# Delta-rule attention with its longest convolution as products with diagonal matrices and its level 0 written down directly, unused products at TensorE's waits, and the first block of keys loaded and projected in halves

## The reference

```python
q = short_conv_silu(hidden_states @ Wq, conv_q_w)   # causal, 4 taps per column; k and v alike
beta = sigmoid(hidden_states @ Wb)
q, k = l2norm(q), l2norm(k); v = v * beta; kb = k * beta
attn = -(kb @ k.T) * strict_lower
for i in range(1, chunk):                            # forward substitution: (I + A)^-1
    attn[i, :i] += attn[i, :] @ attn[:, :i]
u = (attn + eye) @ v
delta_out = ((q @ k.T) * incl_lower) @ u
outs = [dwconv_causal(v_direct, w) for w in (ms_w3, ms_w15, ms_w31)]   # 3, 15 and 31 taps per column
ms_out = (concat(outs) @ kernel_mix_w) @ channel_mixer_w
gate_features = concat([hidden_states, mean|ms_out|, mean|delta_out|, mean|v_direct|])
logits = gelu(gate_features @ fusion_w1 + fusion_b1) @ fusion_w2 + fusion_b2
wts = softmax(logits over the 3 branches)
o = wts0 * ms_out + wts1 * delta_out + wts2 * v_direct
return (o * rsqrt(mean(o * o)) * o_norm_w) @ Wo
```

## Time and profile before

| | |
|---|---|
| median of 3 executions | 2513.3 us (2511.05 to 2516.91) |
| profiled execution, its own time | 2525.92 us |
| its span | 2524.0 us |
| mean granted TensorE clock, share of full speed | 0.926 |
| busy: PE, DVE, ACT, POOL | 90%, 68%, 59%, 16% |

### The profile page before, as it was taken

How to read it: one execution, slowest core, us unless ns; L and a number is a source line. 1 busy time by engine, 2 the same in 40 slices (tenths; PEclk the granted TensorE clock), 3 DMA queues, 4 the chain that set the end, 5 groups by cost and what they waited for, 6 DMA issues and landing times. The chain is left out here.

```text
span 2524.0 us, 67781 instructions
## 1 busy us (share of the span) xinstructions
PE 2276.3 (90%) x26335; PEld 1850.0 (73%) x26335; DVE 1704.4 (68%) x4080; ACT 1485.1 (59%) x2976; POOL 408.0 (16%) x347
## 2 busy tenths in 40 slices
PE   6999999778999999998567899999975999999949
PEld 5888888676777777776543788888854788888738
DVE  5777777437888888887743577777744677777632
ACT  3666666535777777776113366666642666666621
POOL 3222221002212212120000122222102222222000
PEclk9999999888999999999557899999976999999959
DMA  6776676265443443431113766766614766767426
GB/s 137 121 121 119 120 122 106 49 204 149 112 120 92 120 105 103 125 85 42 30 60 107 143 97 117 119 114 118 103 29 110 139 121 119 122 119 121 64 84 209
DMA packets 150490, 277.47 MB, mean 110 GB/s; under 512 B 32654, under 2 KB 70367, under 8 KB 150251
## 3 DMA queue, kind: packets, MB, share of 16 engines
q1 hardware_dynamic: 150252, 274.13, 52.8%
HBM read 118.86 MB, written 0.33 MB: 47 GB/s over the span
## 5 line engine op out<-in xcount | busy, mean ns | idle before, releaser
L1132 DVE TENSOR_REDUCE L3x_tops<-L3x_m_bank 128x1 f32<-128x448 f32 x448 | 262.6, 618 | 126.6 <-PE L3x_m_bank L904 124.3
L1132 DVE TENSOR_REDUCE L2x_tops<-L2x_m_bank 128x1 f32<-128x448 f32 x448 | 262.6, 618 | 123.2 <-PE L2x_m_bank L904 120.8
L454 ACT ACTIVATE L1x_prob<-L1x_p_s,L1x_neg_max 128x512 f32<-128x512 f32 (+1 forms) x400 | 274.9, 687 | 119.4 <-DVE L1x_neg_max L565 116.6
L1132 DVE TENSOR_REDUCE L0x_tops<-L0x_m_bank 128x1 f32<-128x448 f32 x448 | 262.4, 618 | 122.3 <-PE L0x_m_bank L904 120.2
L560 DVE CUSTOM_DVE_ANT_0 L1x_p_s<-L1x_p_s,L1x_mask 128x512 f32<-128x512 f32 (+1 forms) x400 | 273.4, 684 | 37.8 <-PE L1x_p_s L320 32.6
L1037 ACT ACTIVATE L2x_prob<-L2x_s_bank 128x512 f32<-128x512 f32 x448 | 219.4, 542 | 94.3 <-PE L2x_s_bank L915 92.9
L1037 ACT ACTIVATE L0x_prob<-L0x_s_bank 128x512 f32<-128x512 f32 x448 | 219.4, 542 | 91.8 <-PE L0x_s_bank L915 90.6
L1037 ACT ACTIVATE L3x_prob<-L3x_s_bank 128x512 f32<-128x512 f32 x448 | 219.4, 542 | 90.8 <-PE L3x_s_bank L915 89.5
L329 PE MATMUL L1x_p_t<-net_ident,L1x_prob 128*128 128x128 f32 x1568 | 239.7, 274 | 11.7 <-ACT L1x_probT L175 11.6
L329 PEld LDWEIGHTS L1x_p_t<-net_ident,L1x_prob 128*128 128x128 f32 x1568 | 192.9, 141 | 49.7 <-ACT L1x_probT L175 13.5
L320 PE MATMUL L1x_p_s<-L1x_k_stack,L1x_q_stack 96*128 96x512 f32 (+1 forms) x400 | 182.7, 458 | 1.8 <-DVE L1x_q_stack L544 1.8
(11 more groups left out here) (720 smaller groups left out, 4494.6 us busy)
## 6 DMA issues: line engine op xcount, KB each, us to landing
L0x_k_stack<-L0x_kT SPq DMA_DIRECT2D x336, 112.0 KB, 4.0
L2x_k_stack<-L2x_kT SPq DMA_DIRECT2D x336, 112.0 KB, 4.0
L3x_k_stack<-L3x_kT SPq DMA_DIRECT2D x336, 112.0 KB, 4.0
L1x_k_stack<-L1x_kT SPq DMA_DIRECT2D x288, 128.0 KB, 2.4
L3f_w<-in_L_ffn_w SPq DMA_DIRECT2D x16, 1024.0 KB, 9.3
L0x_ctx<-in_ctxT SPq DMA_DIRECT2D x14, 896.0 KB
L2x_ctx<-in_ctxT SPq DMA_DIRECT2D x14, 896.0 KB
L3x_ctx<-in_ctxT SPq DMA_DIRECT2D x14, 896.0 KB
```

The costliest lines, as they stand in the source:

```text
L454: e.activation(prob[:, h % P_RING, 0:nk], p_s[h % S_RING][:, 0:nk], ACT.Exp, bias=neg_max[:, odd, h:h + 1]).then_inc(sem("exped"), 1)
L1132: e.tensor_reduce(tops[:, b % 2, h, half:half + 1], m_bank[n % RING][:, 0:HALF], AX, ALU.max).then_inc(sem("m_free"), 1)
```

## The change

It has three parts. In what follows line numbers of the changed kernel are given only where an order of instructions is shown.

**The delta-rule attention.**
- K is projected first, then V, then Q; Wk comes by SP, Wv and Wq by DMAs that ACT issues after its square root. K and V are convolved on DVE as before, Q on POOL with 7 TENSOR_TENSORs of 256 elements per partition. K is normed alone before the levels, Q within them (levels 2 and 3); the local matrix is made in level 5.
- The 31-tap convolution leaves DVE. POOL spreads the taps into 62 diagonal matrices `diag` (4 TENSOR_TENSORs of 2048, 1920, 2048 and 1920 elements per partition), and PE adds up 62 products of a diagonal matrix with the shifted `vpad` in one bank. They are placed between the other products of the levels. DVE keeps 18 taps, spread 1, 1, 2, 4, 5, 5 over the levels.
- Level 0 has no products: `XT = I - BT`, turned once by PE for `X`. Six levels remain. The copy to `Y` goes from DVE to ACT. `X` is updated, and the next `B·X` released, once `X·Y` alone is there. The last level makes no `X`.
- The `fw1` products (8, with one product of zeros to open the bank) move from the tail into level 1. Gelu is followed piece by piece by its `fw2` product, and the means of sizes are made one by one.

**Unused products.** `keep_busy` multiplies the identity with itself, n times 128x128, into a bank that nobody reads at the time, ahead of a wait of PE: 4 + 9 in each turned cross attention's prologue, 4 + 7 in L1x, 4 + 6 + 5 in L0a and L2a, 4 + 3 + 8 in L0f, 4 + 6 + 3 in L1f, 4 + 6 + 20 + 8 in L1a, 4 + 5 + 12 + 8 in L2f, 14 + 4 + 9 in L3a, 4 + 10 in L3f.

**The prologue of the turned cross attention.** Block 0 comes by two DMAs of 448 keys and is split in halves; the pieces are projected in the order 0, 2, 1, 3, the first two when the first half is split. The split of wv moves from ACT and DVE to POOL, ahead of the split of block 1. Three of the six `k_stack` DMAs of quad 0 of block 0 are issued by ACT, three stay with SP.

```diff
@@ turned cross attention, SP, POOL, PE, ACT, DVE
-                elif b:
-                    e.wait_ge(sem("ctx_0_split"), 1)
...
-                    for r in range(2):
+                    for r in range(1 if b == 0 and j == 0 else 2):
...
-            load(0)
+            for half in range(2):
+                keys = slice(half * HALF, (half + 1) * HALF)
+                e.dma_start(ctx[:, :, keys], ctx_dram[:, :, keys]).then_inc(sem(f"ctx_0_loaded_{half}"), 16)
...
+            e.wait_ge(sem("v_weights"), 16)
+            e.tensor_copy(wv_part[:, HIGH], wv).then_inc(sem("v_weights_high"), 1)
...
             split_ctx(1)
...
+            keep_busy(e, p_oT, ident, 9)
             e.wait_ge(sem("k_weights_split"), 1)
-            e.wait_ge(sem("ctx_0_split"), 1)
-            for i, bank in enumerate([p_proj] + m_bank):
-                project(0, i, bank)
+            for n, bank in enumerate([p_proj] + m_bank):
+                e.wait_ge(sem("ctx_0_split"), 1 + n // 2)
+                project(0, FIRST_KEYS[n], bank)
...
+            e.wait_ge(sem("k_split"), 4)
+            for n, (_, part) in enumerate(PRODUCTS):
+                at, of = GROUP + HD * n, HD
+                e.dma_start(k_stack[at:at + HD, 0, 0::4, :].bitcast(F32),
+                            kT[of:of + HD, 0, part].bitcast(F32)).then_inc(sem("k_stacked_0_0"), 16)
@@ helper
+def keep_busy(e, bank, ident, n):
+    for _ in range(n):
+        e.matmul(bank[:, 0:P], ident[:], ident[:], start=True, stop=True)
@@ delta_rule_attention, POOL
+            def spread_taps(g):
...
+                e.tensor_tensor(diag[:, c, at:at + n, :], ident[:].unsqueeze(1).broadcast_to([P, n, P]),
+                                taps[2][:, c, at:at + n].unsqueeze(2).broadcast_to([P, n, P]),
+                                ALU.mult).then_inc(sem("diag_made"), 1)
+            e.wait_ge(sem("taps_loaded"), 16)
+            spread_taps(0)
...
+            e.wait_ge(sem("pre_copied"), 3)
+            for j in range(4):
...
+                    link(e.tensor_tensor(tapped[:], src, over, ALU.mult))
+                    link(e.tensor_tensor(conv[:, Q], conv[:, Q], tapped[:], ALU.add))
...
+            for g in range(1, 4):
+                spread_taps(g)
@@ delta_rule_attention, PE
+            def spread(first, last):
+                for k in range(first, last):
...
+                    t = e.matmul(bank[5][:, c * P:(c + 1) * P], diag[:, c, j, :], vpad[:, c, j:j + P],
+                                 start=j == 0, stop=j == TAPS[2] - 1)
...
+            keep_busy(e, bank[7], ident, 20)
+            e.wait_ge(sem("k_activated"), 1)
...
-            for level in range(LEVELS):
-                e.wait_ge(sem("B_masked"), level + 1)
+            for level in range(1, LEVELS):
...
+                    e.wait_ge(sem("X_updated"), level - 1)
...
+                if level < LAST:
+                    for h in range(NH):
+                        t = e.matmul(bank[1][:, h * P:(h + 1) * P], XT[:, h, :], Y[:, h, :], start=True, stop=True)
+                    t.then_inc(sem("XBX_made"), 1)
...
+                if level == 1:
+                    e.wait_ge(sem("loop_weights"), LOOP)
+                    e.matmul(bank[7][:], nothing[:, 0:P], nothing[:], start=True, stop=False)
+                    for oc in range(HC):
...
@@ delta_rule_attention, ACT and DVE
+                e.wait_ge(sem("BX_made"), level)
+                e.copy(flat(Y), bank[4][:]).then_inc(sem("BX_copied"), 1)
...
-                e.wait_ge(sem("XBX_made"), level + 1)
-                e.wait_ge(sem("XBXT_made"), level + 1)
-                link(e.tensor_tensor(flat(X), flat(X), bank[1][:], ALU.subtract))
+                if level < LAST:
+                    e.wait_ge(sem("XBX_made"), level)
+                    e.tensor_tensor(flat(X), flat(X), bank[1][:], ALU.subtract).then_inc(sem("X_updated"), 1)
+                e.wait_ge(sem("XBXT_made"), level)
+                e.tensor_tensor(flat(XT), flat(XT), bank[0][:], ALU.subtract).then_inc(sem("XT_updated"), 1)
```

More of the change, by code:

```diff
@@ L1786, in _ @@
[L1786 to L1796 removed]
+            e.wait_ge(sem("k_weights"), 16)
@@ L1856, in _ @@
[L1856 to L1861 removed]
+            e.wait_ge(sem("k_convolved"), 1)
+            e.activation(act[:, K], conv[:, K], ACT.Sigmoid).then_inc(sem("k_sigmoid"), 1)
+            e.wait_ge(sem("v_convolved"), 1)
@@ L1881, in _, with short_taps @@
             e.tensor_copy(flat(xnT), bank[0][:, 0:D]).then_inc(sem("xnT_copied"), 1)
-            e.wait_ge(sem("first_weights"), FIRST)
-            for i in range(3):
-                e.wait_ge(sem("pre_copied"), i + 1)
-                for j in range(4):
+            e.wait_ge(sem("short_loaded"), 16)
+            short_done = 0
+            def short_taps(i, first, last):
+                nonlocal short_done
+                for j in range(first, last):
                     for c in range(DC):
@@ L1944, in convolve @@
+            e.wait_ge(sem("even_masked"), 1)
+            e.wait_ge(sem("odd_masked"), 1)
+            e.tensor_tensor(XT[:], ident[:].unsqueeze(1).broadcast_to([P, NH, P]), BT[:, 0], ALU.subtract).then_inc(sem("first_XT"), 1)
+            e.wait_ge(sem("AT_copied"), 2)
+            e.tensor_tensor(BT[:, 1], AT[:], mask(1), ALU.mult).then_inc(sem("first_B_masked"), 1)
+            every_tap = [(s, j) for s in range(2) for j in range(TAPS[s])]
+            ms_done = 0
             def convolve(first, last):
-                for k in range(first, min(last, len(every_tap))):
+                nonlocal ms_done
+                e.wait_ge(sem("vpad_made"), 1)
+                for k in range(first, last):
```

444 lines of the change are left out of this document (298 added, 146 removed).

## The result

| | before | after |
|---|---|---|
| median | 2512.63 us (2511.05 to 2516.91, 4 executions) | 2475.52 us (2463.77 to 2480.31, 4 executions) |
| profiled execution's span | 2524.0 us | 2478.5 us |
| mean granted clock | 0.926 | 0.956 |
| busy PE / DVE / ACT / POOL | 90 / 68 / 59 / 16% | 93 / 68 / 60 / 17% |

The ratio is 0.9834, 95% interval 0.9805 to 0.9864: faster by 37 us by the medians and 42 by the ratio, where 2472 was forecast with a range of 2446 to 2494. In a later comparison, with 5 executions of the change beside 11 of before, it was 0.9849 (0.9811 to 0.9886).

A forecast was written before the change was run, and what follows sets the result against it. Small modules were taken as chains of short steps handing over between engines, PE often at 1.2 GHz. L1a −18.2, unused products −17.7 and prologues −5.3 sum to −41.2 us: median 2472, range 2446 to 2494.

The forecast's parts named there:

- L1a's levels: Six delta-rule levels of L1a: PE itself bounds them at the full clock, 33 us instead of 58.5, gain 25.5.
- L1a's front: L1a before level 1: POOL's operations block DVE, so level 1 starts at 1238.5 instead of 1222.2, 16.3 us lost.
- L1a's tail: L1a after the levels: smaller hidden layer 6, gelu overlapping fw2 1, higher PE clock 2; gain 9 us.
- Small modules: Unused products in L0a, L0f, L1f, L2a, L2f, L3a, L3f raise PE's clock for the steps behind them; gain 17.7 us.
- L3a's 4: In L3a, the gain forecast from a higher PE clock behind unused products: 4 us.
- L3f's 1.1: In L3f, the gain forecast from a higher PE clock behind unused products: 1.1 us.
- Prologues: Starts of the four cross attentions: L0x and L3x gain 2.3 each, L1x 1.1, L2x loses 0.4; together −5.3 us.
- The three DMAs less on SP: In L0x's prologue, likewise L3x: three fewer SP issues for quad 0 save 2.5 us before the waves' first product.
- A: Rival for L1a's front: POOL does not hold DVE up; level 1 at 1219 or about 1222, total 2454 us; chance 0.16.
- B: Rival: PE stays at 1.2 GHz in L1a and small modules, additional matmuls become the bound; 2534 us; chance 0.05.
- C: Rival: the clock rises in L1a's levels alone, small modules give 3 instead of 17.7 us; 2488 us; chance 0.16.
- D: Rival: POOL's diagonal products in L1a's front take 3 ns an element, 6 us more; 2478 us; within the forecast's 0.6.

The follow-up runs named there:

- old_l1a: The change with the whole delta-rule attention of before, without unused products in it; 2500.0 us, ratio 0.9950 to before.
- thin_levels: The change with 49 of the 62 diagonal products left out, so most of the long convolution is missing; 2466.5 us, ratio 0.9805 to before.
- diag_memset: The change with the last three of POOL's four tap spreads replaced by MEMSETs of the same size, leaving out needed work; 2464.5 us, ratio 0.9801 to before.
- no_busy: The change without any of its unused products; 2483.0 us, ratio 0.9875 to before.
- quad_first: The change with SP's three key DMAs for quad 0 of block 0 issued ahead of the wait for the mask's DMA; 2477.3 us, ratio 0.9846 to before.

## Why the prediction was right, and where its terms were off

The sum was −41.2 us. Measured were −37 (the medians), −42 (the ratio) and −45.5 (the two spans). It came this close by errors that partly cancel, which is luck: L1a gave 25.7 us in the traces and 25 to 29 by old_l1a where 18.2 were forecast, the rest of the change 13 (6 to 19) where 23 were.

- **L1a's levels**: 33 us forecast, 32.0 measured (1223.81 to 1255.78), at a clock of 1.00. That PE itself bounds the levels, with 22 to 24 matmuls at 0.223, is what the trace shows. thin_levels adds that the chain alone would be 3.7 to 3.9 us, forecast as 4. That the clock would rise was right; the reason given, that the levels leave PE no pause, is not needed, since it stood at 1.00 without most of the diagonal products as well.
- **L1a's front**: +16.3 forecast, +8.4 measured. The mechanism stands: POOL's products hold DVE's operations for their whole length (diag_memset). Its sizes were off. "2.2 to 2.3 ns an element" was too much for POOL's diagonal products: 3.61 us for 2048 elements is 1.76, so the four took 14.0 instead of 17.8 us, and the stretch of the last three 10.4 instead of 14.3. The row used had an fp32r output and two full inputs, these have broadcast ones and fp32; which of the two matters no run shows. Q's seven operations took 5.3 us instead of 7.1. And DVE was through with V's taps when POOL ended, where the forecast had five left; from there to level 1 it took 10.9 us, not 13.7, of which 2.7 are K's turn waiting for the eight unused products.
- **L1a's tail**: −9 forecast, −7.7 measured. Gelu's table load, 1.28 us, has come onto the path, which the forecast did not name.
- **Small modules**: −17.7 forecast, −9.3 in the two traces. The mechanism is shown for L0a, L2a and L2f, which lose 2.5 to 3 us without the copies; 6.2 were forecast for them, 7.4 measured. For L0f, L1f, L3a and L3f (11.5 forecast, 1.9 measured) no gain is shown. L3a's 4 and L3f's 1.1 are the terms that are too large: L3a took 27.0 to 32.1 us in twelve traces with copies and 31.1 before, L3f 73.8 to 76.8 in ten and 73.8 before. L1f's −0.4 is one execution; in six traces it was 5 us shorter than before, but before has a single trace, and no_busy is at 65.4.
- **Prologues**: −5.3 forecast, −11.7 in the two traces, of which nothing is certain. The three DMAs less on SP were counted as 2.5 us of the path; quad_first shows that the mask's copy stands beside them and leaves 1.5 at most.
- **The rivals**: A is excluded by the 12.35 us and diag_memset. B is excluded by the clock of 1.00. C, that the small modules give only 3, does not fit L0a, L2a and L2f, though for the other four it is not excluded; that a long wait is what loses the clock there is not shown. D had the wrong sign.
- **Readings**: the cross attentions are 2106 us of the span by the table of modules, not some 2090, which changes nothing in the sum. And the prediction reads the blocking more widely than it is: a GpSimd operation that only writes did not hold DVE (diag_memset).

## What to carry to other kernels

When work is moved to an idle GpSimd, look at what the receiving time costs VectorE: here a GpSimd operation that reads SBUF held every VectorE operation with two SBUF inputs that met it, and sometimes a cast with one. ScalarE (0.31 us a matrix) did the same work in more instructions and without that cost. Filler products ahead of a wait paid where TensorE's next step followed them closely (2.5 to 3 us in each of three modules), and cost where they were still running when the input was there (2.7 us in L1a); elsewhere no gain could be shown. And before a few microseconds of a long module are explained from one trace, a second trace of the same kernel tells whether they are there at all.
